# The second norm's weight moved into the slots, and the token tile made by ScalarE

## The reference

```
h1  = tokens after attention
x   = (h1 - mean) / sqrt(var + 1e-5)                  # _layernorm
xn  = x * rsqrt(mean(x*x) + 1e-5) * norm_weight       # _rms_norm
tok = xn / max(|xn|, 1e-5)
sl  = slots / max(|slots|, 1e-5) * scale
logits = sl . tok                                     # 64 x 324
dispatch_w = softmax over tokens; combine_w = softmax over slots
y = dispatch_w . xn                                   # 64 x 192, then the experts' two layers
out = combine_w . y
```

## Time and profile before

| | |
|---|---|
| median of three runs | 2918.97 us |
| the profiled execution: its own time, and its span | 2921.78 us, 2920.0 us |
| busy: PE, PEld | 2694.3 us, 1976.1 us |
| busy: DVE, ACT, POOL | 1737.9 us, 1549.9 us, 950.7 us |
| mean granted clock of TensorE | 0.968 of full speed |

### The profile page before, as it was taken

One profiled execution on the slowest core, in us unless ns is written; L12 is line 12 of the kernel. 1 busy time (PEld: TensorE's weight loads), 2 busy tenths in 40 slices (PEclk: granted clock), 3 DMA queues, 4 the chain that ended last, 5 costly groups with the idle time before them and its releaser, 6 DMA issues. The chain is left out here.

```text
span 2920.0 us, 72392 instructions
## 1 busy us (share of the span) xinstructions
PE 2694.3 (92%) x25078; PEld 1976.1 (68%) x25078; DVE 1737.9 (60%) x7898; ACT 1549.9 (53%) x3185; POOL 950.7 (33%) x1814
## 2 busy tenths in 40 slices
PE   6799999999999999999999999999999998699955
PEld 5577777777777777777777777777777775355522
DVE  7466666666666666666666666666666665211133
ACT  2466666666666666666666666666666654111100
POOL 3333333333333333333333333333333332000000
PEclk8899999999999999999999999999999997699988
DMA  4333333333333333333333333333333321699988
GB/s 108 94 96 93 95 99 99 99 98 98 98 96 98 98 97 98 97 96 97 98 98 97 96 98 94 96 94 96 95 94 95 99 81 40 191 318 319 290 240 286
DMA packets 380043, 355.46 MB, mean 122 GB/s; under 512 B 37820, under 2 KB 345021, under 8 KB 379678
## 3 DMA queue, kind: packets, MB, share of 16 engines
q1 hardware_dynamic: 342310, 292.68, 36.1%
q10 hardware_dynamic: 37368, 58.15, 6.4%
HBM read 194.45 MB, written 40.30 MB: 80 GB/s over the span
## 5 line engine op out<-in xcount | busy, mean ns | idle before, releaser
L996 DVE CUSTOM_DVE_ANT_0 ps<-ps,late 128x325 f32<-128x325 f32 (+2 forms) x2304 | 748.5, 395 | 7.9 <-PE ps L474 4.0
L719 ACT ACTIVATE prob<-ps 128x590 f32<-128x590 f32 x768 | 500.8, 660 | 182.4 <-PE ps L497 168.0
L431 PE MATMUL ps<-window_w,xp 108*98 108x193 f32 x2304 | 497.4, 334 | 0.6 <-DVE window_w L953 0.6
L474 PE MATMUL ps<-kst,qst 99*128 99x325 bf16 (+2 forms) x2304 | 330.8, 253 | 38.3 <-DVE negmax L996 31.4
L431 PEld LDWEIGHTS ps<-window_w,xp 108*98 108x98 f32 x2304 | 335.8, 165 | 3.7 <-issue 1.5
L474 PEld LDWEIGHTS ps<-kst,qst 99*128 99x128 bf16 (+1 forms) x2304 | 199.7, 106 | 184.0 <-DVE negmax L996 136.7
L996 DVE DVE_READ_ACCUMULATOR2_ANT negmax<- 128x1 f32 (+1 forms) x2304 | 317.3, 138 | 0.0
L513 PE MATMUL ps<-prob,vaug 128*32 128x324 f32 (+2 forms) x4608 | 285.6, 340 | 0.0
L672 PE MATMUL ps<-xt,wqk 97*128 97x324 f32 (+1 forms) x768 | 251.9, 451 | 1.7 <-ACT xt L719 1.7
L491 PE MATMUL ps<-qst,kst 102*128 102x295 bf16 x768 | 228.8, 298 | 25.4 <-ACT prob L719 22.4
L1188 POOL TENSOR_TENSOR rot<-by 128x324 f32<-128x324 f32 x64 | 56.4, 881 | 599.4 <-DVE by L1095 599.4
(11 more groups left out here) (215 smaller groups left out, 5599.1 us busy)
## 6 DMA issues: line engine op xcount, KB each, us to landing
xw<-in_x_dram SPq DMA_DIRECT2D x384, 189.0 KB
qst<-part SPq DMA_DIRECT2D x768, 60.8 KB
w<-in_L_ffn_fc_weight_dram ACTq DMA_DIRECT2D x32, 1152.0 KB, 10.5
kst<-part SPq DMA_DIRECT2D x384, 81.0 KB
w<-in_L_ffn_fc_weight_dram SPq DMA_DIRECT2D x32, 768.0 KB, 8.7
h_held<-h_new SPq DMA_DIRECT2D x64, 288.0 KB, 3.7
kst<-part SPq DMA_DIRECT2D x768, 20.2 KB
w<-in_L_ffn_fc_weight_dram SPq DMA_DIRECT2D x64, 192.0 KB, 10.7
```

The source lines that it names most:

```text
L431: mm = pe.matmul(ps[0:TILE, BK7, half * (D + 1):(half + 1) * (D + 1)], xp[:, q, TILE * half:TILE * (half + 1)], window_w[:, q, :], start=( ...
L474: mm = pe.matmul(ps[0:nq, bk, col:col + keys], qst[i][0:MAX_ROW, h, q0:q0 + nq], kst[i][0:MAX_ROW, h, 0:keys], start=True, stop=True)
L719: return nc.scalar.activation(out_, in_, f, **kw)
L996: last = dve.tensor_tensor_reduce(out=ps[0:nq, bk, col:col + keys], in0=ps[0:nq, bk, col:col + keys], in1=late[0:nq, gone:gone + keys], sc ...
```

## The change

The norm's weight leaves z. Slots are multiplied by it once, before the loop, so that the logits come out the same, and so is `kinds`, the mask by which the slots' inputs are stored into `y_all`; both need the weight before the loop, once as a row (`nwb`) and once as a column (`nw_col`), and its loads stand further ahead in ScalarE's queue. z is now (h1 - mean) * alpha, made by three Identity activations of ScalarE with `alpha` as scale and `less` = -mean * alpha as bias; GpSimd makes `less`. The sum of squares still needs the weighted tokens: GpSimd multiplies z by the weight into `zw` (the buffer `xhat`), text tokens first, and ScalarE squares `zw`, now behind the copies of the transposed z. `beta_t` is max(zss, 1e-10)^-0.5 without alpha, and `disp` is a plain copy.

```diff
@@ -740,8 +741,11 @@
                         for dst, src in ((ns, nscale), (nb, nbias)):
                             act.dma_start(dst[:], src.rearrange("(c p) -> p c", c=2),
                                           allow_slow_non_contiguous=True).then_inc(attn_in, 16)
-                        for dst, src in ((sl, slots), (scl[:], scale.rearrange("(s o) -> s o", o=1)), (ident[:], ident_c)):
+                        for dst, src in ((sl, slots), (scl[:], scale.rearrange("(s o) -> s o", o=1)), (ident[:], ident_c),
+                                         (nwb[:], vector_row(nw).broadcast_to((128, D)))):
                             act.dma_start(dst, src).then_inc(slot_in, 16)
+                        for dst, src in ((nw_col[:, 0:1], nw[0:128]), (nw_col[0:NS, 1:2], nw[128:D]), (nw_col[NS:128, 1:2], nw[128:D])):
+                            act.dma_start(dst, src.rearrange("(p o) -> p o", o=1)).then_inc(slot_in, 16)
                         act.wait_ge(pool_cleared, 1)
                         load_taps(act, offsets, beta, offsets_in)
                         for n in (3, 4):
...
@@ -790,19 +794,28 @@
                                ACT.Copy).then_inc(v_ready.sem, 1)
                         if moe:
 
-                            act.drain()
-                            z_ready.wait(act, b - 1)
-                            beta_ready.wait(act, b - 2)
+                            less_ready.wait(act, b - 1)
+                            ym_mm.wait(act, b - 2)
                             for t, (_, nt) in enumerate(TTILES):
-                                if t > 0:
-                                    act.drain()
-                                last = fn(lexp[0:nt].rearrange("p t s -> p (t s)"), z[0:nt, t, :], ACT.Square,
-                                          accum_out=zss[0:nt, t:t + 1])
-                            last.then_inc(zs_ready.sem, 1)
+                                last = fn(z[0:nt, t], h1[0:nt, t], ACT.Identity, bias=less[0:nt, t:t + 1],
+                                          scale=alpha[0:nt, t:t + 1])
+                            last.then_inc(z_ready.sem, 1)
                         if moe:
                             zt_mm.wait(act, b - 1)
                             fn(zt[:, 0], ps[0:HALF, BK5, 0:T], ACT.Copy)
                             fn(zt[:, 1], ps[0:HALF, BK4, 0:T], ACT.Copy).then_inc(zt_ready.sem, 1)
+                        if moe:
+
+                            beta_ready.wait(act, b - 2)
+                            for n, (t, (_, nt)) in enumerate(((2, TTILES[2]), (0, TTILES[0]), (1, TTILES[1]))):
+                                if n == 0:
+                                    zw_ready.wait(act, b - 1, 1)
+                                else:
+                                    act.drain()
+                                    zw_ready.wait(act, b - 1)
+                                last = fn(lexp[0:nt].rearrange("p t s -> p (t s)"), zw[0:nt, t, :], ACT.Square,
+                                          accum_out=zss[0:nt, t:t + 1])
+                            last.then_inc(zs_ready.sem, 1)
                         if front:
                             strips_mm.wait(act, b + 2)
                             squares_mm.wait(act, b + 1)
...
@@ -932,7 +945,11 @@
                         dve.drain()
                         dve.reciprocal(sn[:], sn[:])
                         dve.drain()
-                        dve.tensor_scalar(sl, sl, sn[:, 0:1], scl[:, 0:1], ALU.mult, ALU.mult).then_inc(slot_ready, 1)
+                        dve.tensor_scalar(sl, sl, sn[:, 0:1], scl[:, 0:1], ALU.mult, ALU.mult)
+                        for c in range(2):
+                            dve.tensor_scalar(kinds[:, c], kinds[:, c], nw_col[:, c:c + 1], None, ALU.mult)
+                        dve.drain()
+                        dve.tensor_tensor(sl, sl, nwb[0:NS], ALU.mult).then_inc(slot_ready, 1)
 
                         dve.wait_ge(first_read, 1)
                         dve.wait_ge(gains_in, 16 * TAP_PIECES)
...
@@ -998,15 +1015,6 @@
                                         in1=late[0:nq, gone:gone + keys], scale=-1.0, scalar=-MASKED, op0=ALU.add, op1=ALU.min,
                                         accum_out=negmax[0:nq, q, h:h + 1])
                                 last.then_inc(max_ready.sem, 1)
-                            if moe and h == 1:
-
-                                ln2_ready.wait(dve, b - 1)
-                                ym_mm.wait(dve, b - 2)
-                                zs_ready.wait(dve, b - 2)
-                                for t, (_, nt) in enumerate(TTILES):
-                                    last = dve.scalar_tensor_tensor(out=z[0:nt, t], in0=h1[0:nt, t], scalar=mv2[0:nt, t, 0:1],
-                                                                    in1=nwb[0:nt], op0=ALU.subtract, op1=ALU.mult)
-                                last.then_inc(z_ready.sem, 1)
                             if moe and h == 9:
 
                                 l_scaled.wait(dve, b - 1)
...
@@ -1059,13 +1067,13 @@
                         if moe:
                             d_mm.wait(dve, b - 1)
                             for n, t0, t1 in GROUPS:
-                                last = dve.tensor_tensor(disp[0:n, t0:t1], ps[0:n, BK4, NS * t0:NS * t1].rearrange(
-                                    "p (t s) -> p t s", s=NS), alpha[0:n, t0:t1].unsqueeze(2).broadcast_to(
-                                    (n, t1 - t0, NS)), ALU.mult)
+                                last = dve.tensor_copy(disp[0:n, t0:t1], ps[0:n, BK4, NS * t0:NS * t1].rearrange(
+                                    "p (t s) -> p t s", s=NS))
                             last.then_inc(dp_ready.sem, 1)
                         if front:
                             rstd2_ready.wait(dve, b + 2)
                             xt_mm.wait(dve, b + 1)
+                            zs_ready.wait(dve, b - 1, apart=True)
                             for t, (_, nt) in enumerate(TTILES):
                                 last = dve.tensor_scalar(xhat[0:nt, t], h_new[i][0:nt, t], mv1[0:nt, t, 0:1],
                                                          rstd2[0:nt, t:t + 1], ALU.subtract, ALU.mult)
...
@@ -1146,20 +1154,19 @@
                         if moe:
 
                             ln2_ready.wait(pool, b - 1)
-                            dp_ready.wait(pool, b - 2)
                             pool.tensor_scalar(alpha[:], mv2[:, :, 1], 1.0 + EPS, EPS * EPS, ALU.mult, ALU.add)
                             power(alpha[:], alpha[:], neg_half[:])
+                            pool.tensor_scalar(less[:], mv2[:, :, 0], -1.0, 0.0, ALU.mult, ALU.add)
                             pool.drain()
-                            pool.tensor_tensor(pw[:], alpha[:], alpha[:], ALU.mult)
-                            pool.drain()
+                            pool.tensor_tensor(less[:], less[:], alpha[:], ALU.mult).then_inc(less_ready.sem, 1)
+                            z_ready.wait(pool, b - 1)
+                            pool.tensor_tensor(zw[:, 2], z[:, 2], nwb[:], ALU.mult).then_inc(zw_ready.sem, 1)
+                            pool.tensor_tensor(zw[0:TILE, 0:2], z[0:TILE, 0:2], nwb[0:TILE].unsqueeze(1).broadcast_to((TILE, 2, D)),
+                                               ALU.mult).then_inc(zw_ready.sem, 1)
 
                             zs_ready.wait(pool, b - 1, apart=True)
-                            pool.tensor_tensor(pw[:], zss[:], pw[:], ALU.mult)
-                            pool.drain()
-                            pool.tensor_scalar(pw[:], pw[:], 1e-10, 0.0, ALU.max, ALU.add)
-                            power(pw[:], pw[:], neg_half[:])
-                            pool.drain()
-                            pool.tensor_tensor(beta_t[:], pw[:], alpha[:], ALU.mult).then_inc(beta_ready.sem, 1)
+                            pool.tensor_scalar(beta_t[:], zss[:], 1e-10, 0.0, ALU.max, ALU.add)
+                            power(beta_t[:], beta_t[:], neg_half[:]).then_inc(beta_ready.sem, 1)
                         if att:
                             maxima_parts(b, 0)
                         if mid:
```

More of the change, by code:

```diff
@@ L127, in early_fusion_kernel @@
                 z = tmp("z", [128, 3, D])
-                ynorm = xhat
+                ynorm = zw = xhat
                 xt = tmp("xt", [HALF + 1, 2, KEYS])
@@ L156, in early_fusion_kernel @@
                 zss, alpha, beta_t = tmp("zss", [128, 3]), tmp("alpha", [128, 3]), tmp("beta_t", [128, 3])
-                pw = tmp("pw", [128, 3])
+                less = tmp("less", [128, 3])
                 neg_half, eps = (tmp(n, [128, 3]) for n in ("neg_half", "eps"))
@@ L165, in early_fusion_kernel @@
                 disp = tmp("disp", [128, 3, NS])
-                kinds = tmp("kinds", [128, 2, NS])
+                kinds, nw_col = tmp("kinds", [128, 2, NS]), tmp("nw_col", [128, 2])
                 RUN = PATCH * 5 * C
@@ L250, in early_fusion_kernel @@
```

(13 more changed lines are left out.)

## The result

The changed kernel takes 2969.13 us (median of 4 runs, 2967.46 to 2970.22), against 2921.97 us for the kernel before (4 runs, 2916.89 to 2925.01). The ratio is 1.0163 (95% interval 1.0144 to 1.0181): slower by 1.6%, outside the predicted range. The profiled executions differ by 47.1 us: 2920.0 us of span before, 2967.1 after.

What follows compares the result with a forecast made beforehand. TensorE was taken as the bound, by short gaps between its groups. The profiled 2921.78 us + 0.0 for the steps + 1.0 start + 1.8 end + 0.6 thin steps gave 2925.2, less 2.8 to the median: 2922, range 2902 to 2942.

Steps and rivals of the forecast that it cites:

- z goes to ScalarE, behind GpSimd: Scores half: three ScalarE activations for z take 0.88 us; TensorE's transposes of z start 0.32 us later than before.
- The first rival: GpSimd's chain to the first maxima is late, each 0.1 us costing 6.1; with 0.35 us, 2943 us; chance 0.28.
- Step against step the sum is 0.00: Transposes of the first maxima: GpSimd's chain lets them start at 1230.21, as before, so a step's length stays the same.
- TensorE's own pace: Heads 4 to 6: head 5 about 0.04 us earlier relative to head 4, head 6 another 0.13.
- rival 4: GpSimd's `less` product takes 1.03 us in place of 0.19, z 0.84 later: 51 us more, 2973; chance 0.03.
- The weighting: GpSimd's two multiplications by the norm's weight, about 0.55 and 0.92 us, don't hold up the Squares; 0.4 to spare.
- the rule behind this: VectorE with two SBUF inputs and GpSimd reading SBUF exclude each other; with a single SBUF input VectorE doesn't contend.
- rival 3: VectorE truly bounds the scores half, so its 1.07 us a step comes back whole: 2857 us; chance 0.05.
- Rival 2: GpSimd's chain gains 0.13 us or more, TensorE runs at its own pace: 2914 to 2895, middle 2905; chance 0.20.
- Start and end: Once-only costs: 1.0 us at the start for VectorE's products on `kinds`, 1.8 in the last step for later z and Squares.
- What would show it: Signs: step 37.3 us, give or take 0.1; wrong if head 9 starts over 0.15 from 7.0 us behind head 3.

Runs made afterwards that it cites:

- the last version: The changed kernel with z = h1 - mean (bias alone), alpha back in `disp`, `beta_t` with a sum for the maximum: 2887.63 us, ratio to before 0.9885.

## Why the prediction was wrong

**The step that failed** stands in "z goes to ScalarE, behind GpSimd": ScalarE "makes three activations of the Squares' width", at 0.88 us for the three. They take 1.42. The Square has immediates (constants in the instruction) for scale and bias, the Identity two operands in SBUF, and each costs 0.093 us: 3 x 2 x 0.093 = 0.56, measured 0.54. The first rival named "an Identity dearer than a Square without its sum" and left it at 0.1 or 0.35 us; it was readable. The kernel before has two activations on the same 64x324 from PSUM, of which one takes a bias per partition (it is an exponential with its sum, the other a copy, so the pair is a hint and no more):

```profile
L719 ACT ACTIVATE dexp<-ps,dmax 64x324 f32<-64x324 f32 x64 | 33.7, 526 | 74.5 <-DVE dmax L1019 74.5
...
L719 ACT ACTIVATE comb<-ps 64x324 f32<-64x324 f32 x64 | 27.8, 435 | 14.2 <-PE ps L637 14.2
```

526 - 435 = 91 ns. The Trainium skill has the rule in ScalarE: Activation LUTs, section What ACT_TABLE_LOAD costs: an activation's fixed part grows by about 93 ns for each operand read per partition. The traces agree: 92 and 93 ns at 192 columns. By these two rows the three activations would have been estimated at 1.43 us in place of 0.88, and the sum at 0.55 x 61 = 34 us more, 2956; by the skill's 93 ns the estimate is the same within 1 us.

**The base step was not typical.** 37.33 was read from one interval; the median is 37.18. In the sampled one z and the maxima's transposes are 0.14 later than in the others; the transposes of z stand within 0.01 of +0.56 in 58 of the 63. So "Step against step the sum is 0.00" compared a forecast of places with a late step. Without operands the places came as forecast (+0.99 for 1.02, +6.77 for 6.75), and the step was still 0.15 longer than the median of before: 9 us. Reading all 63 intervals would have shown it. Together: 0.54 + 0.15 of the 0.73 to 0.75 us a step. With the operands priced right the forecast would still have been some 13 us low.

**Right.** GpSimd's chain became what TensorE waits for at the first maxima (61 waits; the added power came through there whole), and each 0.1 us by which the operands delay z costs a step 0.1. TensorE's own pace between head 4 and head 6 is right too: head 5 comes 0.06 and head 6 another 0.14 us earlier relative to head 4, by the medians, for the forecast 0.04 and 0.13; the wait for GpSimd's parts takes it back. `less` is short, 193 to 195 ns in all 64 steps, where alpha squared took 1.03 us beside VectorE and 192 to 1240 over the steps, 890 by the median: rival 4 is out. The weighting takes 0.59 and 1.00 us for the priced 0.55 and 0.92, within 10 ns in all 64 steps, the last with VectorE idle among them, and hides. The prediction's wording of the rule behind this is too wide, though: a VectorE instruction with a single SBUF tensor, 64x192, took 3.00 us while GpSimd's memsets of `qst` ran (24.78 to 31.51 us). In the Trainium skill, SBUF — State Buffer, section Who interferes with whom, the sentence on one SBUF input is limited to VectorE instructions outside the 2-port perf modes. No run here tells which mode this one was in. VectorE now idles among the heads, and nothing comes of it: rival 3, the whole 1.07 back, is out. Its maxima by busy time and idle time before them, after and before:

```profile
L1013 DVE CUSTOM_DVE_ANT_0 ps<-ps,late 128x325 f32<-128x325 f32 (+2 forms) x2304 | 751.7, 394 | 101.2 <-PE ps L475 101.0
```

```profile
L996 DVE CUSTOM_DVE_ANT_0 ps<-ps,late 128x325 f32<-128x325 f32 (+2 forms) x2304 | 748.5, 395 | 7.9 <-PE ps L474 4.0
```

The same work, with 101.2 us of waiting for scores in place of 7.9. Rival 2, the chain early, did not occur. The pieces of GpSimd's chain were sized well; what starts it was not.

**Start and end.** Start +1.0 was priced: the first statistics come 1.42 us later (58.41 us before, 59.83 after), but by the mt copy at 157.7 nothing is left of it. The end, +1.8: from the last mt copy (2468.80 before, 2515.33 after) to the second part (2505.19, 2553.89) it takes 36.39 and 38.56, 2.2 more. The second part is 1.6 us shorter; over these two and seven other runs it takes 406.1 to 414.8.

**"What would show it"** served: head 9 at 7.6 behind head 3 where 7.0, give or take 0.15, was allowed.

## What to carry to other kernels

When an operation moves to another engine, price it with its operands: find a row with the same kind of operand on that engine, or two rows that differ by it alone, before taking the width's price. What a move off a busy engine gives back is set by when the value now arrives, so split the operation (here: centre early, scale where the product is multiplied anyway) until what the path needs depends on as little as possible. Take the step's length from all intervals, and the places within it from a step of median length.

## What the runs showed of the hardware

- An activation's operand of one value per partition costs 92 to 93 ns of ScalarE's time, bias and scale alike, both 185 ns (354, 446, 539 ns at 98x192).
- With two waits of TensorE of 1.14 and 1.22 us in a step, the second beginning 5.5 us behind the end of the first, the granted clock was 0.50 for about 7 us in most steps and 1.00 throughout in a few; in the kernel after, with 1.13 and 0.24, it was 1.00 in 61 of 63 steps. Of the 171 us that one more power cost, about 60 are the wait and the other 110, by difference, go with the clock (an estimate from the steps at full clock).
- A drain on ScalarE ahead of an activation that was ready moved it by 0.18 us (from 0.66 to 0.84 behind the start of the copies ahead of it), and the step by 0.18 to 0.27.
- GpSimd's products: 128x192 in 0.59 us, 98x384 in 1.00, 128x3 in 0.19; the last 0.19 to 1.24 us at the place where VectorE made z with two inputs in SBUF.
- VectorE's row maxima, 0.96 us a head, set the start of the heads 4 to 6 in the kernel before and in the last version.
